# Where a vision-tower kernel's pooling slices stand among its attention heads, with routing three slots earlier and six residual buffers

## What is computed

```python
pooled = x.reshape(B, 12, 14, 16, 14, 16).sum(axis=(3, 5))      # 16x16 patches: the "pooling"
h = einsum('bcij,ce->bije', pooled, channel_weights)            # 196 tokens of 192
h = h + one_head_attention(layernorm(h))
# mixture layer on y = layernorm(h):
probs = softmax(y @ w_router.T)                                 # 4 experts
gate, idx = top_k(probs over tokens, 98)                        # 98 of 196 tokens per expert
# fc1 -> gelu(768) and q, k, v; 12-head attention; fc2; weighted by the gates
h = h + mlp_part + attention_part
```

## Time and profile before

| | us |
|---|---|
| three runs | 1976.71, 1977.30, 1978.36 |
| median | 1977.3 |
| profiled execution | 1970.27 |
| span of its instructions | 1968.5 |

### The profile page before, as it was taken

How to read it: one execution, slowest core, us unless ns; L and a number is a source line. 1 busy time by engine, 2 the same in 40 slices (tenths; PEclk the granted TensorE clock), 3 DMA queues, 4 the chain that set the end, 5 groups by cost and what they waited for, 6 DMA issues and landing times.

```text
span 1968.5 us, 38799 instructions
## 1 busy us (share of the span) xinstructions
PE 1608.9 (82%) x12434; PEld 1287.7 (65%) x12434; DVE 1226.8 (62%) x2822; ACT 845.9 (43%) x1934; POOL 248.9 (13%) x318
## 2 busy tenths in 40 slices
PE   4116289978898799987899789987899788998998
PEld 2004177757686577766777577765787577777786
DVE  2466757684686747685676837776576847563553
ACT  1001065434544345434554345433554346445653
POOL 2002101110022001110021100210011100210000
PEclk8557589978899779987999789987999789999999
DMA  2896646445555435555355446446364442212220
GB/s 72 221 229 163 172 83 143 109 111 132 122 122 113 119 87 137 136 117 136 95 114 134 108 101 149 111 114 159 69 145 116 109 121 50 39 23 41 51 56 15
DMA packets 161084, 218.51 MB, mean 111 GB/s; under 512 B 135099, under 2 KB 149605, under 8 KB 150118
## 3 DMA queue, kind: packets, MB, share of 16 engines
q10 hardware_dynamic: 12288, 154.15, 29.7%
q1 hardware_dynamic: 148582, 61.68, 17.8%
HBM read 186.57 MB, written 28.90 MB: 109 GB/s over the span
## 4 chain that ended last, share of the span: by engine, by line
PE 39%; issue 37%; DMA 9%; DVE 8%; POOL 3%; ACT 2%; SPq 1%; POOLq 0%; DVEq 0%; ACTq 0%
PE bank L952 7%; PE bank L859 7%; DMA xt<-in_x_dram 4%; PE bank L887 4%; PE bank L921 3%; PE bank L869 3%; DMA ks<-qk_scratch 3%; PE bank L906 2%; DVE psums L1211 2%; POOL var L1466 2%; PE bank L767 2%; PE bank L783 2%; DVE peaks L1403 2%; PE bank L734 1%; PE bank L849 1%
## 5 line engine op out<-in xcount | busy, mean ns | idle before, releaser
L1403 DVE TENSOR_REDUCE peaks<-bank 98x2 f32<-98x392 f32 x768 | 425.4, 562 | 318.6 <-PE bank L887 301.3
L1099 ACT ACTIVATE Pb<-bank 98x392 f32<-98x392 f32 x768 | 374.8, 497 | 337.5 <-PE bank L906 285.6
L1211 DVE TENSOR_REDUCE psums<-xt 112x2 f32<-112x512 f32 x672 | 442.6, 679 | 85.1 <-DMA xt<-in_x_dram 52.3
L887 PE MATMUL bank<-ks,qs 96*98 96x196 f16 x1536 | 274.1, 267 | 62.9 <-DVE peaks L1403 40.3
L952 PE MATMUL bank<-w2T,hid 128*98 128x192 f32 x1536 | 306.2, 338 | 0.0
L906 PE MATMUL bank<-qs,ks 97*98 97x196 f16 x1536 | 275.0, 264 | 3.1 <-ACT Pb L1099 2.7
L887 PEld LDWEIGHTS bank<-ks,qs 96*98 96x98 f16 x1536 | 164.8, 130 | 171.7 <-issue 79.5
L952 PEld LDWEIGHTS bank<-w2T,hid 128*98 128x98 f32 x1536 | 244.7, 173 | 2.6
L921 PE MATMUL bank<-Pb,vals 98*32 98x196 f32 x3072 | 186.7, 365 | 5.1 <-DVEq L1397 2.5
L906 PEld LDWEIGHTS bank<-qs,ks 97*98 97x98 f16 x1536 | 173.8, 134 | 17.4 <-issue 9.6
L734 PE MATMUL bank<-spread_p,cst 112*24 112x196 f32 x192 | 49.2, 406 | 127.0 <-POOL spread_p L1457 127.0
(11 more groups left out here) (181 smaller groups left out, 1896.6 us busy)
## 6 DMA issues: line engine op xcount, KB each, us to landing
xt<-in_x_dram ACTq DMA_DIRECT2D x96, 1568.0 KB, 9.1
qk_scratch<-qk SPq DMA_DIRECT2D x64, 294.0 KB, 3.7
qs<-qk_scratch SPq DMA_DIRECT2D x192, 73.5 KB, 3.3
ks<-qk_scratch SPq DMA_DIRECT2D x192, 73.5 KB, 3.6
out_dram<-fin SPq DMA_DIRECT2D x64, 147.0 KB
qs<-shiftT SPq DMA_DIRECT2D x128, 2.3 KB
hid<-in_L_ffn_w_dram SPq DMA_DIRECT2D x1, 1440.0 KB
hid<-in_L_ffn_w_dram SPq DMA_DIRECT2D x1, 960.0 KB
```

The lines of the kernel that those rows point to most:

```text
L887: mm = pe.matmul(peak_ps[s][0:HT, T * q:T * q + T], qs[0:KS, i % NSTACK, h, HT * q:HT * q + HT], ks[0:KS, i % NSTACK, h, :], start=True, s ...
L1099: act.activation(Pb[:, (H * i + h) % NP, :, :].rearrange("p a b -> p (a b)"), score_ps[s][0:HT, 0:2 * T], ACT.Exp, scale=float(DH) ** -0.5 ...
L1211: last = dve.tensor_reduce(psums[:, m % 2, t, 2 * p:2 * p + 2], v[:, 2 * p:2 * p + 2, :, :], AX.XY, ALU.add)
L1403: dve.tensor_reduce(peaks[:, h // 6, :, h % 6], peak_ps[s][0:HT, 0:2 * T].rearrange("p (q k) -> p q k", q=2), AX.X, ALU.max, negate=True). ...
```

## The change

The body is now built as a plan of 104 entries (96 slots and the eight steps of the opening). Routing and turning are put in first, from slot 27 (`TAKE`) instead of 30, with `gates` three places behind `gate_logits` instead of two and a half and `gate_rows` two places behind `gates` instead of one. `evenly` then gives each entry a room of 2.2 us less the VectorE time of the operations that it has (table `VECTOR`) and places the pool slices at equal steps of the summed room: 21 in slots 0 to 22, and 63 from slot 28 to two steps before the end of the opening. `own_row`, `fetch`, `planes` and `tok` follow their slices. `NRES` goes from 4 to 6, and `RESIDUAL` puts images 5, 6 and 7 at slots 34, 41 and 46 instead of 41, 53 and 61. In group 6 and in the prologue only the routing's spacing changes. No operation is added or dropped.

Worked out from the table and the rule, the 84 pool slices of one body stand so:

| entries | before | after |
|---|---|---|
| slots 0 to 27 | 21 | 21 |
| slots 28 to 59 | 26 | 31 |
| slots 60 to 69 | 9 | 7 |
| slots 70 to 83 | 13 | 2 |
| slots 84 to 94 | 10 | 18 |
| slot 95 | 5 | 2 |
| opening | 0 | 3 |

The rounds of `choose` stand at slots 71 to 83 before and 70 to 82 after; `chosen` and `spread` at 85 and 86, and both at 84; the first `turn_u` at 88 and 87. `planes` and `tok` of the last tile stand in slot 95 before; after, in steps 5 and 6 of the opening. The fetch that loads the last tile stands at slot 79 before and 87 after; that tile's first slice at 93 and 94.

```diff
-NRES = 4
+NRES = 6
-def pooling(dg, m, start, pace, more=True):
+def pooling(dg, m, at, more=True):
     ops = []
     for t in range(TILES):
         for p in range(PIECES):
-            slot = start + pace * (PIECES * t + p)
+            slot = at[PIECES * t + p]
             ops.append((slot, ("pool", dg, m, t, p)))
         ops.append((slot + 1, ("own_row", dg, m, t)))
         if more or TILES * m + t + NX < TILES * GRP // PAIR:
             ops.append((slot + 2, ("fetch", dg, m, t)))
-    ops += [(slot + 2.5, ("planes", dg, m)), (slot + 4, ("tok", dg, m))]
+    ops += [(slot + 2.2, ("planes", dg, m)), (slot + 3.4, ("tok", dg, m))]
     return ops
+def evenly(plan, count, first, end):
+    room = [max(ROOM - sum(VECTOR.get(op[0] if op[0] != "fc2" or op[3] == FC2 - 1 else "", 0) for op in ops), 0)
+            for ops in plan[first:end]]
+    upto = np.concatenate([[0], np.cumsum(room)])
+    want = (np.arange(count) + 0.5) / count * upto[-1]
+    where = np.searchsorted(upto, want, side="right") - 1
+    return [first + int(k) for k in where]
-    ops += [(at, ("gate_scale", dg)), (at + 2, ("gate_logits", dg)), (at + 4.5, ("gates", dg)),
-            (at + 5.5, ("gate_rows", dg))]
-    at += 6.5
+    ops += [(at, ("gate_scale", dg)), (at + 2, ("gate_logits", dg)), (at + 5, ("gates", dg)),
+            (at + 7, ("gate_rows", dg))]
+    at += 8
-RESIDUAL = {(0, 5): 0, (0, 10): 1, (1, 5): 2, (1, 10): 3, (2, 5): 4, (3, 5): 5, (4, 5): 6, (5, 1): 7}
+RESIDUAL = {(i // 2, 5 * (i % 2) + 5): i for i in range(GRP)}
+TAKE = 27
+ROOM = 2.2
+VECTOR = {"peak": 0.6, "choose": 1.5, "first_max": 0.6, "take": 1, "norm1_scale": 1, "norm1": 0.8, "shift1": 1,
+          "stream": 1, "stream_norm": 1.2, "gate_scale": 0.3, "gate_logits": 1.8, "gates": 2, "gate_rows": 0.4,
+          "chosen": 0.4, "spread": 3, "project": 1.2, "norm_turn": 0.7, "fc2": 0.8, "gate8": 1.2}
-    pace = 1.1
-    if with_next:
-        for m in range(AHEAD, GRP // PAIR):
-            front += pooling(1, m, pace * TILES * PIECES * (m - AHEAD), pace, pool_next)
-        front += routing(1, 30, 1)
-        front += turning(1, 88)
-    if pool_next:
-        for m in range(AHEAD):
-            front += pooling(2, m, 32 + pace * TILES * PIECES * m, pace)
+    plan += opening(1, True)
+    front = routing(1, TAKE, 1)
+    front += turning(1, max(slot for slot, _ in front) + 2.5)
+    for slot, op in in_slots(front):
+        plan[slot].append(op)
+    pieces = TILES * PIECES
+    at = evenly(plan, pieces * (GRP // PAIR - AHEAD), 0, TAKE - 4)
+    front = []
+    for m in range(AHEAD, GRP // PAIR):
+        front += pooling(1, m, at[pieces * (m - AHEAD):], pool_next)
+    if pool_next:
+        at = evenly(plan, pieces * AHEAD, TAKE + 1, len(plan) - 3)
+        for m in range(AHEAD):
+            front += pooling(2, m, at[pieces * m:])
+    for slot, op in in_slots(front):
+        plan[min(slot, len(plan) - 1)].append(op)
+    return sum(plan, [])
```

More of the change, by code:

```diff
@@ L130, in pooling, with steadily @@
             ops.append((slot + 2, ("fetch", dg, m, t)))
-    ops += [(slot + 2.5, ("planes", dg, m)), (slot + 4, ("tok", dg, m))]
+    ops += [(slot + 2.2, ("planes", dg, m)), (slot + 3.4, ("tok", dg, m))]
     return ops
+def steadily(start, pace):
+    return [start + pace * k for k in range(TILES * PIECES)]
+def evenly(plan, count, first, end):
[5 more added lines that the diff above has]
+    return [first + int(k) for k in where]
 def routing(dg, at, pace):
@@ L172, in turning, with in_slots @@
     return ops + [(at + 1 + 0.5 * i, ("turn_u", dg, i)) for i in range(2, GRP)]
+def in_slots(ops):
+    return [(int(np.floor(slot)), op) for slot, op in sorted(ops, key=lambda o: o[0])]
 def in_order(ops):
@@ L184, in prologue @@
     for m in range(GRP // PAIR):
-        front += pooling(0, m, TILES * PIECES * m, 1)
+        front += pooling(0, m, steadily(TILES * PIECES * m, 1))
     end = TILES * PIECES * GRP // PAIR + 3
@@ L188, in prologue @@
     for m in range(AHEAD):
-        front += pooling(1, m, end + 6 + 0.75 * TILES * PIECES * m, 0.75)
+        front += pooling(1, m, steadily(end + 6 + 0.75 * TILES * PIECES * m, 0.75))
     front += turning(0, end + 60)
-    return ops + in_order(front) + opening(0, False)
+    return ops + in_order(front) + sum(opening(0, False), [])
 def opening(dg, tail):
-    ops = []
+    plan = []
     last = GRP - 1
     for i in range(GRP):
+        ops = []
+        plan.append(ops)
         if tail:
@@ L220, in opening @@
     ops.append(("shift", dg, 0, 1))
-    return ops
-RESIDUAL = {(0, 5): 0, (0, 10): 1, (1, 5): 2, (1, 10): 3, (2, 5): 4, (3, 5): 5, (4, 5): 6, (5, 1): 7}
-def body(pool_next, with_next):
-    ops = []
-    front = []
-    pace = 1.1
-    if with_next:
-        for m in range(AHEAD, GRP // PAIR):
-            front += pooling(1, m, pace * TILES * PIECES * (m - AHEAD), pace, pool_next)
-        front += routing(1, 30, 1)
-        front += turning(1, 88)
-    if pool_next:
-        for m in range(AHEAD):
-            front += pooling(2, m, 32 + pace * TILES * PIECES * m, pace)
-    slots = {s: [] for s in range(H * GRP)}
-    for slot, op in sorted(front, key=lambda o: o[0]):
-        slots[min(int(np.floor(slot)), H * GRP - 1)].append(op)
+    return plan
+RESIDUAL = {(i // 2, 5 * (i % 2) + 5): i for i in range(GRP)}
[4 more added lines that the diff above has]
+          "chosen": 0.4, "spread": 3, "project": 1.2, "norm_turn": 0.7, "fc2": 0.8, "gate8": 1.2}
+def body(pool_next, with_next):
+    plan = []
     for i in range(GRP):
-        fill = [slots[H * i + h] for h in range(H)]
+        fill = [[] for h in range(H)]
         if i:
@@ L269, in body @@
                 ops.append(("mix", 0, i - 1, H // QUAD - 1))
-    if with_next:
-        return ops + opening(1, True)
-    ops.append(("mix", 0, GRP - 1, H // QUAD - 1))
-    ops += [("norm_turn", 0, GRP - 1, half) for half in range(2)]
-    ops.append(("norm_back", 0, GRP - 1))
-    return ops + [("fc2", 0, GRP - 1, k) for k in range(FC2)]
+    if not with_next:
+        plan.append([("mix", 0, GRP - 1, H // QUAD - 1)])
+        plan.append([("norm_turn", 0, GRP - 1, half) for half in range(2)])
+        plan.append([("norm_back", 0, GRP - 1)])
+        plan.append([("fc2", 0, GRP - 1, k) for k in range(FC2)])
+        return sum(plan, [])
[15 more added lines that the diff above has]
+        plan[min(slot, len(plan) - 1)].append(op)
+    return sum(plan, [])
 def ring_of(op):
```

## The result

| | kernel before | kernel after |
|---|---|---|
| median | 1977.4 us (1976.7 to 1978.4) | 1953.1 us (1946.6 to 1958.3) |
| profiled execution, its span | 1970.3, 1968.5 | 1946.6, 1944.8 |
| mean granted clock of TensorE | 0.871 | 0.891 |

The ratio is 0.9875, with a 95% interval of 0.9838 to 0.9912: 24 us less, 1.2%. The forecast was 113 less, 1864 us, and 1953 lies outside its range (1828 to 1910). The direction was right and the size was a fifth of what was forecast.

The account below looks back on a forecast made before the run. TensorE was taken as the bound up to slot 59, VectorE from slot 70 to 83, with idle time and low clock later. Stretches summed to 206.6 us per body, 18.5 less; six bodies plus group 6's 2.3 gave 1864 us, range 1828 to 1910.

Parts of the forecast that it names:

- slot 95 and the opening: End of a body: the wait for planes and the low clock after it go, 42.5 us to 33.1.
- rival A: From slot 85 on VectorE becomes the bound and waits for a late last tile; 1904 us, chance 0.18.
- cross-check: Opening: group 6's 29.7 us plus planes and tok (1.6) and the loop's turn (1 to 2) agrees with 33.1.
- Slots 28 to 69: Three more slices, TensorE stays the bound; 87.1 us to 86, ends 84.5 and 89.
- the earlier places find a free buffer: Slots 28 to 69: with six buffers the residuals' earlier places need no wait; by themselves they cost and gain nothing.
- Rival C: Slots 28 to 47: the clock falls where TensorE is the bound; slower, up to +30.9 us per body, 2050 us, chance 0.06.
- Slots 70 to 83: VectorE loses 11 slices, 25.1 us busy to 17.6; the stretch falls from 29.1 us to 21, gain 8.1.
- Slots 84 to 94: VectorE gains 8 slices and just fits; no gain, 23.6 us to 23.7, ends 21 and 25.4.
- B: Four stretches from slot 28 on: clock stays up and TensorE runs on; 6.6 us less per body, 1824 us, chance 0.10.
- D: Slots from 28 on: the order differs but slices cost the same in new slots; time stays at 1977 us, chance 0.06.

Follow-up runs that it names:

- e2_small: Kernel after, with the two tile loads issued at slots 92 and 95 cut to 8 of 112 rows, nothing moved: 1902.41 us.
- e8_one: Kernel after, with only the second of the two fetches moved, from slot 95 to the opening's step 2: 1904.77 us.
- e4_routing: Kernel after with slices near the old pace and the old pile in slot 95; new routing, spacing, six buffers and residual places kept: 1974.15 us.
- e3_pool: Kernel after with the old routing, spacing, four buffers and residual places; only the slices placed by room: 1971.82 us.
- e1_late: Kernel after, with the last three fetches moved from slots 92 and 95 and step 5 to the opening's steps 2, 4 and 6: 1924.95 us.
- e6_turn: e1_late with its last fetch moved past the turn of the loop, to slot 7 of the next body: 1923.72 us.
- e9_best: Kernel after, with the fetches at the opening's steps 1 and 3, then at slots 8, 14 and 21 of the next body: 1942.44 us.
- e11_pile_turn: e5_pile with the last fetch moved to the next body's slot 7 and the two after it to slots 14 and 21: 2006.29 us.
- e12_pile_clean: e11_pile_turn with the next body's three fetches moved to slots 21, 22 and 33: 1963.99 us.
- e10_tuned: Kernel after, with the last two fetches at the opening's steps 2 and 4, and the fetch of slot 16 at slot 21: 1897.48 us.
- e5_pile: Kernel before, with what is planned behind slot 95 put on the opening's steps instead of onto slot 95, the last fetch at step 6: 1962.43 us.
- e7_turn_before: Kernel before, with its last fetch moved from slot 95 to the opening's step 6: 1993.16 us.

## Why the prediction was wrong

Per body, means of groups 0 to 4 beside the forecast's terms:

| | before | forecast | after |
|---|---|---|---|
| slots 0 to 27 | 43.8 | 42.8 | 43.4 |
| 28 to 69 | 87.1 | 86 | 89.2 |
| 70 to 83 | 29.1 | 21 | 22.1 |
| 84 to 94 | 23.6 | 23.7 | 23.6 |
| 95 and opening | 42.5 | 33.1 | 43.3 |
| body | 226.1 | 206.6 | 221.6 |

Of the 15.0 us that are missing in a body, the opening holds 10.2.

**The step that failed: slot 95 and the opening.** The part on it counted the fetch of the last tile by ScalarE's wait alone, "nothing", and did not count the moved fetches' transfers at all, though the moved step issues them. The transfers met project's last stack loads, and the path from those to TensorE's first peak was left out. e2_small and e8_one price it at 7.3 us per opening (216.4 to 180.0 and 179.9 in five). The prediction had both landing times before it, 3.6 and 9.5 us, and spoke of fetches packed at slots 87, 92 and 95, but under rival A, and with VectorE waiting for a late tile. That did not occur: no slice waited for `xt` there. TensorE waited for a late stack instead. Two errors stand beside it. The landing time of 9.5 is that of a load that landed with the first tile load; with two tile loads issued within 2 us it landed with the second, after 16.5. And a late stack is on TensorE's path at once, where a late tile would have met a VectorE with time to spare. The Trainium skill ("DMA: Bandwidth & Descriptors", section "Issuing engines are not separate DMA queues") says that the starting engine does not matter, since all DMAs interleave on the same 16 DMA engines. The trace agrees: a load of SyncE's takes 3.6 us on the median, 9.3 beside one of ScalarE's in e8_one and up to 16.5 beside two in after.

The rest of the opening: without the collision it takes 36.0 us (e8_one, e2_small) where 33.1 were forecast. The forecast's cross-check put the turn of the loop at 1 to 2 us; its sum carried before's turn, 2.8 on the mean, and in e8_one the turn took 3.8. TensorE also waits once for ScalarE's Pb, 1.29 us in each body. These two are 2.3 of the 2.9 us that are missing. And TensorE is busy for 30.8 us where the sum left it 29.8, which no run takes apart, while before's wait of 0.5 us for `planesT` is gone.

**Slots 28 to 69, forecast 86, measured 89.2.** I took a microsecond off where 2.1 came on top; 89 was the upper end given. e4_routing, with only four slices in slots 28 to 35, has the same 89.3, and e3_pool, without the new routing and residual places, 87.1. So the price is of the half with the routing, and not of the full slots 28 to 35, which I had named as the tightest. The waits of TensorE there that before and e3_pool do not have are `first_exp` for GpSimd's `tm`, and fc2 for ScalarE's `onT`. Group 4 of after, then of e4_routing:

```profile
1244.48 1.63 PE L815 MATMUL bank<-tm,aT 128*98 128x196 f32 x4 [1.38 <-POOL tm L1518]
...
1289.12 0.89 PE L984 MATMUL bank<-w2T,onT 96*98 96x192 f32 x4 [1.26 <-ACT onT L1046]
```

```profile
1260.14 0.91 PE L815 MATMUL bank<-tm,aT 128*98 128x196 f32 x4 [0.99 <-POOL tm L1518]
...
1304.62 0.89 PE L984 MATMUL bank<-w2T,onT 96*98 96x192 f32 x4 [0.94 <-ACT onT L1046]
```

They add up to 2.6 and 1.9 us, about the price; no run took them away, so that they are its cause is read from the trace and not shown. The forecast said that the earlier places find a free buffer, and asked nothing of how late GpSimd and ScalarE would be. The equal means hide a difference: e4_routing took 89.2 or 89.3 in each of the five bodies, at clock 1.00, but after took 88.5 or 88.6 in three and 90.2 in two, where a piece at the low clock (0.95 in slots 48 to 59 above) adds 1.7. Rival C's mechanism, a fall of the clock in the stretch where TensorE is the bound, exists there at a price of 1.7 us, not 31.

**Slots 70 to 83, forecast 21, measured 22.1.** Right in mechanism: VectorE is busy for 18.1 us (17.6 forecast). e3_pool gives 4.2 of the 7.0, e4_routing 1.4, and the whole change gives 1.4 more than the two together.

**Slots 84 to 94.** Right, 23.6. The wait for the last peaks is 3.60 us in group 4, where 3.06 was taken from the earlier trace rows.

**The rival outcomes.** A named the collision but another victim; its 1904 is what e8_one measures without the collision, so the nearness of those two numbers is chance. B and D did not occur, although e4_routing alone is D exactly: its order is different and the time is 1974. By the forecast's own steps, with the opening at 36 in place of 33.1 and slots 28 to 69 at 89.2, the body is 42.8 + 89.2 + 21 + 23.7 + 36 = 212.7. e8_one shows 214.5 (216.7 + 446.1 + 112.0 + 118.0 + 179.9 = 1072.7 in five).

**Account of the whole**, profiled executions, 1968.5 - 1944.8 = 23.7 us: five bodies 22.5, group 5's 3.8, group 6's 2.2; the prologue is 3.5 longer and the end 1.3. The start of the first body lay between 260.5 and 277.2 us in kernels with nearly the same prologue, so its 3.5 can't be put down to the change.

## What to carry to other kernels

When a plan moves compute steps, list the DMAs that move with them and set each beside every small load that the critical engine reads soon: here two tile loads of 1568 KB in the wrong 2 us ate most of the gain, and moving one of them by a few slots brought it back. Keep large loads away from the turn of a hardware loop. After clearing one collision look for the next place where the same load lands, since e1_late, e6_turn, e9_best, e11_pile_turn and e12_pile_clean each moved it to another.

## What the hardware showed that I had not expected

The turn of the loop cost TensorE 2.4 to 3.3 us with no tile load in flight, or one that landed in its first 1.3 us (before, e4_routing, e6_turn, e10_tuned). It cost 3.1 to 4.6 where the load landed 1.5 to 2.9 us into the turn (after, e3_pool, e8_one), and 5.9 to 8.0 where it landed after 3.9 us or more (e1_late, e5_pile, e7_turn_before). Beside two tile loads a stack load of 73.5 KB landed after 16.5 us, for 3.6 on the median, while the tile loads themselves took 10.8 and 14.9, for 8.9: the small load is slowed far more than the large ones. It did not land between them but with the later one, within 0.4 us in all five openings. And one row of 2.3 KB was late enough beside a tile load for TensorE to wait 4.4 us.
